# Windowed attention after a convolutional mixer: both images of a step taken together on each engine, and the second output tile ahead of the third

## What is computed

```python
x = x + _L0_conv_ref(_gn(x), ...)   # outlook attention: 3 x 3 neighbours, 6 heads
x = x + _L1_conv_ref(_gn(x), ...)   # attention in shifted windows of 7 x 7, 12 heads of 16

xw = windows(roll(x, (-3, -3)))                  # 64 windows of 49 tokens an image
q, k, v = split(xw @ qkv_weight.T + qkv_bias)
attn = softmax(q * 16 ** -0.5 @ k.T + rpb + mask)
out = roll(unwindow((attn @ v) @ proj_weight.T + proj_bias), (3, 3))
```

## Time and profile before

| | |
|---|---|
| median of 3 runs | 3687.9 us (3683.56 to 3694.56) |
| profiled execution, its own time | 3694.54 us |
| its span | 3692.7 us |
| granted TensorE clock, mean | 0.949 of full speed |
| PE busy, PE loading weights | 90%, 53% |
| DVE, POOL, ACT busy | 74%, 65%, 51% |
| chain that ended last | PE 44%, POOL 16%, issue 16%, ACT 11%, DVE 8% |
| HBM | 23 GB/s over the span |

### The profile page before, as it was taken

One profiled execution on the slowest core, in us unless ns is written; L12 is line 12 of the kernel. 1 busy time (PEld: TensorE's weight loads), 2 busy tenths in 40 slices (PEclk: granted clock), 3 DMA queues, 4 the chain that ended last, 5 costly groups with the idle time before them and its releaser, 6 DMA issues.

```text
span 3692.7 us, 105251 instructions
## 1 busy us (share of the span) xinstructions
PE 3321.1 (90%) x39908; PEld 1964.0 (53%) x39908; DVE 2743.5 (74%) x4465; ACT 1869.8 (51%) x3602; POOL 2413.9 (65%) x1888
## 2 busy tenths in 40 slices
PE   5999989899899988988889888898989989899988
PEld 3456644566445664456643566346663466634665
DVE  4967779677796777967779677786767867687676
ACT  3445544555435554455543555435554455544555
POOL 2767747676476764767647676477765777566774
PEclk7999989999899998999989999999989999899998
DMA  4732237222371223712246222561215512165122
GB/s 105 141 80 67 73 77 138 65 82 62 84 142 49 83 75 76 143 52 75 76 87 131 64 71 67 105 128 56 83 50 115 121 52 84 55 126 110 56 74 60
DMA packets 204343, 317.51 MB, mean 86 GB/s; under 512 B 16922, under 2 KB 176154, under 8 KB 203802
## 3 DMA queue, kind: packets, MB, share of 16 engines
q0 software_dynamic: 31936, 148.66, 20.7%
q1 hardware_dynamic: 171866, 161.61, 15.0%
HBM read 45.97 MB, written 38.54 MB: 23 GB/s over the span
## 4 chain that ended last, share of the span: by engine, by line
PE 44%; POOL 16%; issue 16%; ACT 11%; DVE 8%; DMA 4%; DVEq 0%; POOLq 0%; SPq 0%; ACTq 0%
POOL sp__70 L1767 6%; POOL sp__70 L1774 4%; PE P L485 4%; DMA prod<-prod 4%; PE P L726 3%; PE P L649 3%; PE P L713 3%; DVE prod L1419 3%; POOL xr L1760 3%; PE P L647 3%; PE P L651 3%; ACT kbd L1095 2%; ACT kbd L1094 2%; DVE sp__70 L1523 2%; PE P L694 2%
## 5 line engine op out<-in xcount | busy, mean ns | idle before, releaser
L1774 POOL TENSOR_TENSOR sp__70<-sp__70,rc 128x588 f32<-128x588 f32 x512 | 600.9, 1174 | 465.1 <-DVE rc L1540 459.2
L1419 DVE TENSOR_TENSOR prod<-P,vpad 128x896 f32<-128x896 f32 (+1 forms) x768 | 791.3, 1051 | 140.1 <-PE P L485 126.7
L1537 DVE TENSOR_REDUCE sm<-sp__70 128x12 f32<-128x588 f32 x512 | 390.8, 763 | 479.7 <-ACT sp__70 L1112 479.6
L1767 POOL TENSOR_TENSOR sp__70<-sp__70,mx 128x588 f32<-128x588 f32 x512 | 598.0, 1173 | 217.8 <-DVE mx L1530 217.6
L1112 ACT ACTIVATE sp__70<-sp__70 128x588 f32<-128x588 f32 x512 | 358.2, 700 | 706.0 <-POOL sp__70 L1767 705.9
L485 PE MATMUL P<-at,sel 108*128 108x448 bf16 x1512 | 429.5, 363 | 63.1 <-DVE prod L1419 32.9
L1523 DVE TENSOR_TENSOR sp__70<-P,relb 128x588 f32<-128x588 f32 x512 | 389.6, 761 | 119.8 <-PE P L713 114.1
L1687 POOL DMA_DIRECT2D prod<-prod x216 | 202.5, 941 | 373.4 <-DVE prod L1419 369.9
L1530 DVE TENSOR_REDUCE mx<-sp__70 128x12 f32<-128x588 f32 x512 | 389.3, 760 | 9.1
L1120 ACT ACTIVATE pt<-P 98x588 f32<-98x588 f32 x512 | 311.7, 663 | 128.6 <-PE P L726 126.7
L726 PE MATMUL P<-ident,sp__70 113*98 113x113 f32 x3072 | 354.2, 267 | 19.5 <-DVE sp__70 L1523 19.5
(11 more groups left out here) (255 smaller groups left out, 7356.9 us busy)
## 6 DMA issues: line engine op xcount, KB each, us to landing
prod<-prod POOLq DMA_DIRECT2D x216, 672.0 KB, 5.6
vbd<-vs SPq DMA_DIRECT2D x512, 147.0 KB
xin<-in_x SPq DMA_DIRECT2D x126, 336.0 KB, 4.2
out<-ot SPq DMA_DIRECT2D x184, 168.0 KB, 3.6
out<-ot SPq DMA_DIRECT2D x80, 84.0 KB
wn<-in_L_conv_qkv_weight SPq DMA_DIRECT2D x2, 432.0 KB, 6.1
wno<-in_L_conv_proj_weight SPq DMA_DIRECT2D x2, 144.0 KB, 6.6
self<-in_sel SPq DMA_DIRECT2D x3, 91.1 KB
```

The source lines that it names most:

```text
L1419: tt(by_row(dst), by_row(P[:, b:b + len(op), 0:CT]), val, ALU.mult).then_inc(prod_ok, 1)
L1537: red(sm[:, b, :], sp_[:, b, :].rearrange("p (h k) -> p h k", h=NH), AX.X, ALU.add).then_inc(p_sum, 1)
L1767: tt(per_head(sp_[:, b, :]), per_head(sp_[:, b, :]), spread(mx[:, b, :]), ALU.subtract).then_inc(t_sub, 1)
L1774: tt(per_head(sp_[:, b, :]), per_head(sp_[:, b, :]), spread(rc[:, b, :]), ALU.mult).then_inc(p_norm, 1)
```

## The change

PE, ACT, DVE and POOL get another order in the rows of the attention stage, and a few waits move with it.

- ACT: in a step both exponentials of the next step (image 0, then image 1) come behind the two copies of probabilities. Before, the one of image 0 was issued at the end of the step before, ahead of the copies.
- POOL: both shifts of the next step come first in a step, a `stage_` piece often behind them, then both normalizations. `stage_norm` moves from steps 0, 1, 2 to steps 1, 1, 2.
- DVE: the statistics come ahead of the sums; in step 2 two `finish` come ahead of both sums, the third stays at the start of step 3.
- `ROW_ORDER` is 0, 1, 2 with banks R0, R2, R1: `end` multiplies the middle tile (R2) first and tile 2 (R1) last. What was the second of three in R1 is now the third. The waits for R1 count one more, among them `fin_ok` ahead of the values.
- PE: `begin` may wait for its banks R0 and R1 between its matmuls (`freed`). The waits for `Y_BANK` (`ot_kept`, `x_kept`) move from before the scores to behind them. The three `turn_next` of a row move from steps 1, 2, 2 to steps 2, 2, 3.
- The residual is made by two operations, times `one` and plus the bias, in place of one.

```diff
+ROW_ORDER, ROW_BANKS = (0, 1, 2), (R0, R2, R1)
...
                     mm(P[HI, bank, 0:n], w[:, 2, col:col + 64], src[:, 2], start=True, stop=False)
+                    if freed is not None:
+                        pe.wait_ge(*freed)
                     mm(a, w[LO, 1, col:col + 128], src[LO, 1], start=True, stop=False)
...
-                    second = mm(b, w[:, 2, col + 64:col + 192], src[:, 2], start=False, stop=True)
-                    return second, mm(P[:, bank, 0:n], mid[:, k, :], src[:, 1], start=False, stop=True)
+                    second = mm(P[:, bank, 0:n], mid[:, k, :], src[:, 1], start=False, stop=True)
+                    return second, mm(b, w[:, 2, col + 64:col + 192], src[:, 2], start=False, stop=True)
...
                     elif p == 1:
+                        end_keys(w + 1)
                         if w >= 2:
                             pe.wait_ge(y_kept, ONE + PAIRS * R + 1)
                             turn_out(w - 2, 3, Y_BANK)
-                        end_keys(w + 1)
-                        pe.wait_ge(k_kept, ONE + T * (R + 1) + 1)
-                        turn_next(w, 0, R0)
-                        if w >= 2:
-                            pe.wait_ge(ot_kept, ONE + NT * (R - 2) + 4)
                     elif p == 2:
+                        end_out(w - 1)
                         pe.wait_ge(y_kept, ONE + PAIRS * R + 2)
-                        turn_next(w, 1, Y_BANK)
-                        end_out(w - 1)
+                        turn_next(w, 0, Y_BANK)
                         pe.wait_ge(fin_ok, ONE + T * (R - 1) + 1)
-                        turn_next(w, 2, R0)
-                        pe.wait_ge(x_kept, x_count + 2)
+                        turn_next(w, 1, R0)
...
+                def y_bank_free(w, p):
...
+                    if w >= 2 and p < 2:
+                        pe.wait_ge(ot_kept, ONE + NT * (R - 2) + 2 * (p + 1))
+                    elif w >= 1 and p >= 2:
+                        pe.wait_ge(x_kept, x_count + (1 if p == 2 else 3))
...
                     elif p == 1:
-                        pe.wait_ge(k_kept, ONE + T * (R + 2))
-                        pe.wait_ge(x_kept, x_count + 1)
-                        begin_out(w - 1)
+                        pe.wait_ge(k_kept, ONE + T * (R + 1) + 2)
+                        begin_out(w - 1, freed=(k_kept, ONE + T * (R + 2)))
                     elif p == 2:
-                        pe.wait_ge(fin_ok, ONE + T * (R - 1) + 2)
-                        pe.wait_ge(x_kept, x_count + 3)
+                        pe.wait_ge(fin_ok, ONE + T * (R - 1) + 3)
+                        pe.wait_ge(x_kept, x_count + 2)
                         window_values(w + 1, 0)
...
                             scores(w2, p2)
+                        if w < NW - 1:
+                            y_bank_free(w, p)
                         attend(w, p)
...
-                pe.wait_ge(k_kept, ONE + T * NW * i + 2)
+                pe.wait_ge(k_kept, ONE + T * NW * i + 3)
                 begin_queries(0, EDGE, Y_BANK)
...
                         w1, p1 = pair_after(w, p, 1)
+                        exp_step(w1, p1, 0)
                         exp_step(w1, p1, 1)
                         late(w, p)
-                        w2, p2 = pair_after(w, p, 2)
-                        exp_step(w2, p2, 0)
...
                         w1, p1 = pair_after(w, p, 1)
-                        if w >= 1 and p == 3:
-                            finish(w - 1, 2, R2)
+                        if w >= 1 and p == 2:
+                            finish(w - 1, 0, ROW_BANKS[0])
+                            finish(w - 1, 1, ROW_BANKS[1])
+                        elif w >= 1 and p == 3:
+                            finish(w - 1, 2, ROW_BANKS[2])
...
                         prob_sum(w1, p1, 0)
-                        if w >= 1 and p == 2:
-                            finish(w - 1, 0, R0)
                         prob_sum(w1, p1, 1)
...
-                    pool.tensor_scalar(by_window(xr[:, w % 2, j, :]), rows(w, j), bout[:, j:j + 1], None,
-                                       ALU.add).then_inc(xr_ok, 1)
+                    pool.tensor_scalar(by_window(xr[:, w % 2, j, :]), rows(w, j), one[:], bout[:, j:j + 1],
+                                       ALU.mult, ALU.add).then_inc(xr_ok, 1)
...
+                        if w == NW - 1 and p == 0:
+                            stage_residual(w, 2)
                         if w1 < NW:
+                            shift_step(w1, p1, 0)
                             shift_step(w1, p1, 1)
-                            normalize_step(w1, p1, 0)
```

More of the change, by code:

```diff
@@ L122, in mixer @@
         fence = sb("fence", [128, 1])
+        one = sb("one", [128, 1])
         mv = sb("mv", [128, T, 2])
@@ L642, in first_queries, with begin @@
                     middle(bank, wt, 0, 0, src, n).then_inc(qh_mm, 1)
-                def begin(banks, bank, w, col, src, n):
+                def begin(banks, bank, w, col, src, n, freed=None):
                     a, b = P[:, banks[0], 0:n], P[:, banks[1], 0:n]
@@ L665, in end_queries, with begin_keys @@
                     third.then_inc(q_mm, 1)
[L667 to L668 removed]
+                def begin_keys(w, lo=0, freed=None):
+                    begin((R0, R1), R2, wt, C, xw[:, w % 2, :, lo:RT], RT - lo, freed).then_inc(k_mm, 1)
                 def end_keys(w, lo=0):
@@ L673, in end_keys, with begin_out @@
                     third.then_inc(k_mm, 1)
-                def begin_out(w, banks=(R0, R1), bank=R2):
+                def begin_out(w, banks=(R0, R1), bank=R2, freed=None):
                     pe.wait_ge(y_kept, ONE + PAIRS * (NW * i + w + 1))
-                    begin(banks, bank, wot, 0, yt[:, w % 2, :, :], RT).then_inc(out_mm, 1)
+                    begin(banks, bank, wot, 0, yt[:, w % 2, :, :], RT, freed).then_inc(out_mm, 1)
                 def end_out(w, banks=(R0, R1), bank=R2):
@@ L1250, in _ @@
                 keep_keys(0, 0, R0, EDGE)
-                keep_keys(0, 1, R1, EDGE)
                 exp_step(0, 0, 1)
-                keep_keys(0, 2, R2, EDGE)
-                for n, bank in enumerate((R0, R1, Y_BANK)):
+                keep_keys(0, 1, R2, EDGE)
+                keep_keys(0, 2, R1, EDGE)
+                for n, bank in enumerate((R0, Y_BANK, R1)):
                     keep_queries(0, n, bank, EDGE)
-                exp_step(0, 1, 0)
                 for m in range(2):
@@ L1591, in last_row @@
                     w, Gn = NW - 1, CHUNKS * (i + 1)
+                    stat_x(i + 1, w - 2, range(T))
                     prob_sum(w, 1, 0)
                     prob_sum(w, 1, 1)
-                    stat_x(i + 1, w - 2, (1, 2))
                     ahead(w, 0)
@@ L1608, in last_row @@
                     coefficients(2 * i + 2)
-                    finish(w - 1, 1, R1)
-                    finish(w - 1, 2, R2)
+                    finish(w - 1, 1, ROW_BANKS[1])
+                    finish(w - 1, 2, ROW_BANKS[2])
                     prob_sum(w, 3, 0)
@@ L1622, in last_row @@
                     finish(w, 0, R1)
-                    finish(w, 1, R2)
-                    finish(w, 2, Y_BANK)
+                    finish(w, 1, Y_BANK)
+                    finish(w, 2, R2)
                 score_bias(0, 0, 0)
@@ L1653, in _ @@
             pool.memset(self32[:], 0.0).then_inc(zeroed, 1)
+            pool.memset(one[:], 1.0)
             pool.memset(eps_s[:], EPS).then_inc(zeroed, 1)
+            pool.wait_ge(zeroed, 4)
             def bias_tiles(dst, v):
```

81 lines of the change are left out of this document (40 added, 41 removed).

## The result

The changed kernel takes 3878.3 us, the median of 4 runs (3867.02 to 3883.93). The kernel before took 3691.2 in the same comparison, so the ratio is 1.0499, with a 95% interval of 1.0458 to 1.0540: slower by 184 us by the ratio (187 between the medians), where the prediction had 107 (3795.0 against 3687.9). The profiled execution took 3867.02 us, its span 3865.2, at a mean granted clock of 0.928 (0.949 before).

A forecast was written before the change was run, and what follows sets the result against it. TensorE's order of work was taken to bound a row, with ScalarE's queue adding some 2.6 us. Per pair 14.0 + 1.1 + 1.1 - 3.0 = +13.2, eight pairs +106, giving 3795 us, range 3740 to 3860 (0.68).

The forecast's parts named there:

- The stand: In step 2, TensorE's value matmuls wait for VectorE's third `finish`: 3.1 to 3.6 us, about 48 times, some 160 us.
- Step 1 at 8.0: Second of a row's four steps: one transposition leaves, ScalarE's queue of copies is late next; 8.0 us, from 10.89.
- Step 2 at 10.7: Third step of a row: values wait for the third `finish`, behind bias adds and maxima; 10.7 us, from 7.17.
- Step 0 ... 7.2: First step of a row: the 0.71 us gap for `ot` ahead of the scores goes; 7.2 us, from 7.98.
- Step 3: 8.1: Last step of a row: one transposition more, +0.4, and a 0.3 gap ahead of the second values gone; 8.1 us.
- The clock at 2.2 us a row: After the 3.5 us stand the granted clock falls in every row, costing 2.2 us; ends 0 and 3.4.
- rival (a): The clock holds through the stall in step 2: 3688 us, no change; chance 0.08.
- Row 0 at +1.1: First row of a pair: first windows' queries wait for the third key tile instead of the second, two copies, +1.1 us.
- The residual at nothing: GpSimd's residual drops from 1284 to 684 ns, 115 us of its time, but gains nothing more for the kernel.
- Rival (c): Step 1's three waits drop the clock a second time: +67 to +106, about 3880 us; chance 0.13.
- (b): Rival: the clock holds, the stall is at its lower end and step 1's waits close: 3613 us; chance 0.08.
- (d): Rival: GpSimd is the bound, and 115 us of its residuals come back: 3680 us, no change; chance 0.03.

The follow-up runs named there:

- e7: The changed kernel with the third `finish` moved to step 2, between the two sums, and the first half of the `vbd` issues ahead of SyncE's wait: 0.9665 of before.
- e2: The changed kernel with SyncE issuing the first half of the `vbd` transfers ahead of its wait for the last `xin` transposition: 1.0357 of the kernel before.
- e4: The changed kernel with 13 idle matmuls of constants ahead of the values' wait for `fin_ok`: 1.0193 of the kernel before.
- e3: The changed kernel with its second output tile `finish`ed second from R1 again, and the first half of the `vbd` issues ahead of SyncE's wait: 0.9683 of before.
- the repaired kernel: The kernel of e3, the changed kernel with both repairs: 0.9683 of the kernel before.
- e6: The kernel of e3 with the residual back to one operation: 0.9657 of the kernel before.
- e5: The kernel before with only the residual changed, to two operations: 0.9833, 62 us faster.
- e9: The kernel before with only ScalarE's order changed, both exponentials of the next step behind the probability copies: 1.0133 of the kernel before.

## Why the prediction was right in kind and wrong in size

- **The stand, right.** "Some 160 us in all", 48 times, 3.1 to 3.6 each: 157.4 us, 48, at most 3.3. Its cause, the third `finish` behind the bias adds, is shown by e7, which moves that one instruction and changes nothing else against e2.
- **Step 1 at 8.0, right.** It is 8.0 in every kernel made from the changed one, and the granted clock of step 1 is 1.00 in all rows 1 to 6 of the change.
- **Step 2 at 10.7, 0.2 too long.** 10.50 with the clock high (e4), -10 us over 48 rows.
- **"Step 0 ... 7.2": the step that failed.** TensorE alone needs 7.2, as e2 and e3 show, but only the gap for `ot` was looked at. The third `turn_next` had been moved to step 3, and the part on step 3 counted it as 0.4 us of TensorE. Its other effect was left out: SyncE waits for it, and eight transfers, 7 us of issuing, stand behind that wait. "The other moved instructions cost the same as before" covered no queue but TensorE's. Measured: 8.18 instead of 7.28 in step 0, and 52 us by the ratio of e2 (33 to 71). It is the largest single term of the miss; without it the time would have been about 3826 (3843 by the profiled executions), inside the range of 3740 to 3860.
- **"Step 3: 8.1", too short, by a misreading.** It is 8.43 in the mean with the clock high (e4; 8.47 in the row shown): 0.35 x 48 = 17 us. The gap of 0.3 did vanish, as no wait for `vs` is left in the list. But the sum started from 8.07, with the end of the row read at 1345.65; the trace has 1345.85 and 8.27, and 8.27 + 0.4 - 0.3 makes 8.4.
- **The clock at 2.2 us a row, nearly right.** Measured 2.35 (e4), +7 us. That it falls in every row was the right choice against rival (a). The size was partly luck: the same misreading made the cost of the short stretch 1.36 us, where the steps 1 of two rows, one with the stretch and one at full clock, differ by 1.56 and the other steps by 0.05 at most:

```profile
1319.52:1330.41 10.89, 8.96 (x131) 5.24 (x129) 6.93 (x13) 7.27 (x13) 7.68 (x8) 0.84 0.03 9
1219.17:1228.50 9.33, 7.40 (x131) 4.82 (x129) 6.39 (x12) 7.27 (x13) 6.27 (x7) 1.00 0.04 12
```

TensorE was busy for 3.39 of those 3.40 us, so next to nothing of that stretch was "hidden behind waits", as the prediction put it. By the Trainium skill ("TensorE: Matmul & The Clock Gate", Terms), throttled time times one minus the ratio, 6.80 us at half would be 3.4; the row shows 2.68. Half of the 5.53 us in which TensorE was busy in that stretch makes 2.77, an estimate that fits: for the other 1.27 us it had nothing to run. For the short stretch of 3.40 us the same rule gives 1.70 against 1.56.
- **Row 0 at +1.1, too little.** The wait for the third key tile is 2.53 us, and the clock falls behind it: the way from the first keys to row 0 is at least 1.4 us longer (17.6 before, 19.0 to 22.7 after), about 3.2 by the traces, which makes +17 us for 8 pairs above what was counted.
- **Last row at -3.0**: right. The group means start 11.7 us into the row, predicted 12.0, where they started at 15.1 in the row that was read; the third step ends 2.7 us sooner.
- **Row 1 at +1.1, too little.** Its 35.2 is measured at 35.2, but the 34.06 it was held against was one row; the mean of before is 33.4.
- **The bounds** "about 3640 to 3900" don't follow from the two terms named: clock 0 to 3.4 and last row 0 to -5 put into the same sum give 3672 to 3875.
- **The residual at nothing**: right in the repaired kernel (e6), whose rows are 6.6 us shorter than those of the change and leave GpSimd less room, but for a reason that would not carry. The same edit in the kernel before is worth 62 us (e5), although no wait of TensorE in the attention stage names GpSimd there.

The corrections, 52 + 17 + 7 + 17 - 10 = 83 us, stand against a miss of 77 (184 - 107), but the first alone is uncertain by 19, so the fit proves little. The two profiled executions close by themselves. Against before, a pair is 20.2 us longer in rows 2 to 6, 1.8 in row 1, 0.2 in row 0 and 3.2 on the way to it, and 3.9 shorter from the start of row 7 to the first keys of the next pair: 21.5, in eight pairs 172, as their spans differ (3865.2 - 3692.7). The prediction had 14.0, 1.1, 1.1 for the third and fourth together, and -3.0: so 50 us of the miss lie in rows 2 to 6, where step 0 alone is 0.98 above its 7.2 in 40 rows, 39 us. Rival (c), a second fall of the clock, gave about the measured time, 3880, for the wrong reason: the clock falls once in a row, for longer (in one row of 48 a second time, in step 0), and step 1 has no low stretch. (b) falls with the clock, and (d) with the measured time: the residuals are shorter, and the kernel is slower all the same.

What stays open: why row 1 and the last row gain so much in e5, and which parts of the change make the repaired kernel faster than before; e5 and e9 test two of them in the kernel before, and neither result carries over by itself.

## What to carry to other kernels

When a step that frees a bank or signals a semaphore is moved later, follow every queue that waits for the signal, the DMA queue first, and count what is issued behind that wait; here 0.4 us of TensorE moved by one step delayed eight issues, 7 us of SyncE's queue. When the order of tiles in banks changes, look where the freeing instruction stands in the other engine's queue, and move it with the order. A stand of TensorE of some 3 us can cost 1.6 to 1.7 times its length (2.85 + 2.35 for 3.3 over all; 5.6 in a plain row, from 36.38 in e2 to 30.76 in e3), since the clock goes with it; if it can't be removed, matmuls of constants in it give back the clock's part.

## What the runs showed of the hardware

- Thirteen matmuls of constants (2.98 us) in a stand of 3.24 kept the granted clock at 1.00 over both steps, where without them it was 0.50 for 6.80 us from within the stand on; 113 us of 3878 came back, though the values started no sooner.
- What the list of waits doesn't name can still have a price: GpSimd's residual was named by no wait of TensorE in the attention stage and was worth 62 us in the kernel before, nothing in the repaired order. For the waits that it did name, list and price can't be told apart here: `vbd` 33.2 us against 33 to 71, the stand 3.3 us a row against 3.2 in a plain row.
- GpSimd's scalar operation on 128 x 392 float32 took 1284 ns with one operation (add) in the kernel before, 1283 in e6, and 687 with two (multiply, add) in the change.
- Eight issues of `vbd<-vs` occupy SyncE's queue for 7 us, 0.82 to 0.92 each (3.30 / 4 in e2, 7.36 / 8 before), so what stands behind them in the queue is held for as long.
